# Adding the constant of the variance: a sum over pairs with a preset area in place of an addition with a scalar

## The reference, cut to what matters

```
def _layernorm(x, w, bias):
    mu = mean(x, -1);  var = mean(square(x - mu), -1)
    return (x - mu) * rsqrt(var + EPS) * w + bias          # EPS = 1e-5
def step(h):
    h = h + 0.01 * tanh(h)
    h = h * sigmoid(h)
    h = _layernorm(h, ln_w, ln_b)
    return einsum('bsc,dc->bsd', h, W) + b
x = x + scan(step, _layernorm(x), length=30)
```

## Time and profile before

| what | us |
|---|---|
| median of 3 runs (lowest, highest) | 1390.7 (1389.99, 1391.48) |
| the profiled execution's own time | 1390.53 |
| its span on the core | 1388.6 |
| DVE line 1116 in that span, 240 instructions | 107.3 busy, 0.447 each |

### The profile page before, as it was taken

How to read it: one execution, slowest core, us unless ns; L and a number is a source line. 1 busy time by engine, 2 the same in 40 slices (tenths; PEclk the granted TensorE clock), 3 DMA queues, 4 the chain that set the end, 5 groups by cost and what they waited for, 6 DMA issues and landing times.

```text
span 1388.6 us, 28231 instructions
## 1 busy us (share of the span) xinstructions
PE 1332.4 (96%) x8786; PEld 1085.0 (78%) x8786; DVE 1234.2 (89%) x2774; ACT 1011.1 (73%) x1373; POOL 948.3 (68%) x749
## 2 busy tenths in 40 slices
PE   4899999999999999869999999999999999999998
PEld 3677777777777776558888888888888888888887
DVE  6678888887788886599999999999999999999997
ACT  1344444444444444569999999999999999999994
POOL 2244444444444444269999999999999999999995
PEclk9899999999999999969999999999999999999999
DMA  5111111111111100000000000000000000000004
GB/s 178 39 39 38 38 38 38 38 38 38 38 38 38 37 0 1 0 1 0 0 0 0 0 0 0 0 0 0 0 0 0 0 0 0 0 0 0 0 0 122
DMA packets 29790, 27.68 MB, mean 20 GB/s; under 512 B 3269, under 2 KB 21448, under 8 KB 29640
## 3 DMA queue, kind: packets, MB, share of 16 engines
q1 hardware_dynamic: 29768, 27.41, 6.2%
HBM read 23.21 MB, written 4.19 MB: 20 GB/s over the span
## 4 chain that ended last, share of the span: by engine, by line
PE 78%; DVE 11%; issue 4%; ACT 3%; POOL 1%; SPq 1%; DMA 0%; DVEq 0%; ACTq 0%; POOLq 0%
PE psum L751 34%; PE psum L763 15%; PE psum L747 6%; PE psum L553 4%; PE psum L555 4%; PE psum L554 4%; PE psum L694 3%; PE psum L570 2%; PE psum L575 2%; ACT emb_f L855 2%; PE psum L584 2%; DVE emb_n L1177 1%; DVE x_less_n L1161 1%; PE psum L564 1%; DVE xh L1059 1%
## 5 line engine op out<-in xcount | busy, mean ns | idle before, releaser
L751 PE MATMUL psum<-w_t,y_all 128*128 128x128 f32 x3840 | 493.7, 282 | 0.0
L751 PEld LDWEIGHTS psum<-w_t,y_all 128*128 128x128 f32 x3840 | 447.9, 192 | 54.5 <-issue 54.5
L454 POOL TENSOR_TENSOR f_rs<-f_var,half_neg 128x8 f32<-128x8 f32 x240 | 410.4, 1710 | 49.2 <-DVE f_var L1116 30.2
L1091 DVE BATCH_NORM_STATS2 f_stat<-g_ring 128x6 f32<-128x256 f32 x960 | 340.7, 413 | 3.9 <-ACT g_ring L813 3.9
L458 POOL TENSOR_TENSOR h_ring<-g_ring,f_rs 128x640 f32<-128x640 f32 x240 | 302.5, 1260 | 18.8
L1107 DVE SCALAR_TENSOR_TENSOR u_ring<-t_ring,psum 128x1024 f32<-128x1024 f32 x232 | 278.1, 1199 | 0.0
L763 PE MATMUL psum<-ident,h_ring 128*128 128x128 f32 x1920 | 250.6, 274 | 6.4 <-DVE h_ring L1080 6.4
L813 ACT ACTIVATE g_ring<-u_ring 128x1024 f32<-128x1024 f32 x240 | 253.5, 1056 | 0.8 <-DVE u_ring L1107 0.8
L836 ACT ACTIVATE y_all<-psum 128x1024 f32<-128x1024 f32 x240 | 243.7, 1015 | 8.4 <-PE psum L763 8.4
L822 ACT ACTIVATE t_ring<-psum 128x1024 f32<-128x1024 f32 x232 | 238.6, 1029 | 13.5 <-PE psum L751 4.9
L763 PEld LDWEIGHTS psum<-ident,h_ring 128*128 128x128 f32 x1920 | 219.1, 142 | 7.1 <-issue 3.8
(11 more groups left out here) (158 smaller groups left out, 1774.3 us busy)
## 6 DMA issues: line engine op xcount, KB each, us to landing
work<-in_adj_dram SPq DMA_DIRECT2D x16, 1024.0 KB, 5.4
x_tok<-in_x_dram SPq DMA_DIRECT2D x16, 256.0 KB, 5.5
out_dram<-y_all SPq DMA_DIRECT2D x8, 512.0 KB, 3.3
work<-in_L_gnn_conv_w_dram SPq DMA_DIRECT2D x1, 1088.0 KB
work<-in_L_gnn_w_ih_dram SPq DMA_DIRECT2D x1, 384.0 KB
work<-in_L_gnn_w_hh_dram SPq DMA_DIRECT2D x1, 192.0 KB
work<-in_L_gnn_W_dram SPq DMA_DIRECT2D x1, 64.0 KB, 5.1
work<-in_L_ffn_weight_dram SPq DMA_DIRECT2D x1, 64.0 KB, 4.8
```

The costliest lines, as they stand in the source:

```text
L454: pool.tensor_tensor(f_rs[:, j % 4, :], f_var[:, j % 2, :], half_neg[:, 0:GT], ALU.pow).then_inc(f_pow, 1)
L751: m = pe.matmul(y_ps[k % 2][:, h, C * t:C * t + C], y_all[:, GT * k + NT * h + t, :], w1_t[:], start=False, stop=True, skip_group_check=True)
L1091: ins = dve.bn_stats(f_stat[:, j % 2, q, :], both)
```

## The change

The statistics area gets a second half of the same shape. At the start of the kernel the whole area is set to 128 * EPS (`C * EPS`), one more memset of 96 values per partition. The statistics instructions write only the first half, so the second keeps the constant. In each slot the addition with a scalar is replaced by a sum over the innermost axis of length 2: it reads, for each of the 8 tiles, the third value of the first half and the preset value of the second half, 16 values in all, and writes 8. The waits, the semaphores and the place in the order stay as they are.

```
-        f_stat = sb("f_stat", [P, 2, GT // 2, 6])
+        f_stat = sb("f_stat", [P, 2, 2, GT, 3])
...
             dve.memset(half_neg[:], -0.5)
+            dve.memset(f_stat[:], C * EPS)
...
-                        ins = dve.bn_stats(f_stat[:, j % 2, q, :], both)
+                        ins = dve.bn_stats(f_stat[:, j % 2, 0, 2 * q:2 * q + 2, :].rearrange("p t w -> p (t w)"), both)
...
-                    squares = f_stat[:, j % 2, :, :].rearrange("p q (o w) -> p (q o) w", w=3)[:, :, 2]
-                    dve.tensor_scalar(f_var[:, j % 2, :], squares, C * EPS, None, ALU.add).then_inc(f_v, 1)
+                    squares = f_stat[:, j % 2, :, :, 2].rearrange("p o t -> p t o")
+                    dve.tensor_reduce(f_var[:, j % 2, :], squares, AX_X, ALU.add).then_inc(f_v, 1)
```

## The result

| | before | after |
|---|---|---|
| median of the runs, us | 1391.09 (4 runs, 1389.99 to 1391.65) | 1380.37 (4 runs, 1379.24 to 1381.05) |
| the profiled execution, us | 1390.53 | 1381.05 |
| its span, us | 1388.6 | 1379.1 |

The ratio is 0.9923, its 95% interval [0.9906, 0.9940]: 10.7 us less, with 8.3 to 13.1 as the interval. The forecast was 1381.2.

The account below looks back on a forecast made before the run. A closed loop of POOL and DVE was taken to bound the kernel. From 1390.53, 27 x (25.765 - 25.42) = -9.3, rounded to -9.4, memset 0: 1381.1; the median 0.17 above: 1381.2 us, range 1379.5 to 1387.0.

Parts of the forecast that it names:

- TensorE's pace, seen in iteration 2, as the floor: Iterated stage: without waiting for DVE, TensorE runs every iteration at 25.42 us, 3.178 a slot, in place of 25.765.
- The hold by line 458: DVE's `f_var` addition waits until POOL's product (line 458) is over, 0.30 us of its 0.38 interval.
- The sum is not held, and takes 0.163 us: The new sum of 16 values on DVE passes beside line 458, held part 0, length 0.163 us.
- The first rival: The sum on DVE is held as the addition was: slot stays 3.24, 1391 to 1393 us, chance 0.10.
- The loop of POOL and DVE sets 25.76 us: The two engines wait for each other: seven slots of 3.24 us and one of 3.08 make the 25.76 us iteration.
- The hold passes to `h_ring`: DVE's `h_ring` (line 1080), behind the sum, is now held by line 458; DVE's slot becomes 2.94 to 3.12 us.
- POOL's loop at 3.05, between 2.94 and 3.17: POOL's power no longer waits for a held instruction, so POOL's slot is 3.05 us, under TensorE's 3.178.
- the second rival: Only part comes: POOL's power still waits some 0.15 us behind line 458, 1382 to 1390 us, chance 0.13.
- the third: Rival: POOL's power (line 454) queues behind both `h_ring` instructions, making it slower, 1399 us, chance 0.06.
- the lock-out: Rival: `h_ring` starting just as line 458 starts loses 1.1 us; if every second slot, about 1450 us, chance 0.01.
- The memset hidden: Start of kernel: 96 more values, 0.1 to 0.2 us, cost 0 behind DVE's 4.40 us wait for a transfer.
- A gain of 9.4 and not 72 us: The 240 holds of 0.30 us don't all count, since PE leaves room for only 0.043 us a slot.

Follow-up runs that it names:

- e3: Kernel before, scalar addition kept but its source laid out as 5 pairs with gaps (10 values): 1381.55 us, ratio 0.9931.
- e1: Kernel before, scalar addition replaced by an addition of two tensors, the statistics and a preset area of 8 values: 1390.23 us, ratio 0.9997.
- e4: Kernel before, scalar addition kept, but POOL's line 458 does 4 of 8 tiles in place of 5, DVE 3: 1380.65 us, ratio 0.9923.
- e8: Changed kernel with a longer sum, 128 values in all: 1391.4 us, ratio 1.0004 to the kernel before.
- e9: Changed kernel with a sum of 64 values in all: 1380.67 us, ratio 0.9923 to the kernel before.
- e5: Kernel before without the two bias products (line 747) on TensorE: 1387.91 us, ratio 0.9975.
- e6: Changed kernel without the two bias products (line 747) on TensorE: 1349.84 us, ratio 0.9705 to the kernel before.
- e12: Changed kernel with bias products moved behind the other 16, only each bank's first product starting a sum: 1371.87 us, ratio 0.9859 to the kernel before.

## Why the prediction was right

- **TensorE's pace, seen in iteration 2, as the floor.** Right to 0.01 us: 25.413 us an iteration from the second on, where the prediction had 25.42. It was the term that made the forecast: 27 x 0.345 = 9.3, taken as 9.4; measured 27 x (25.765 - 25.413) = 9.5. The other 1.2 us of the 10.7 lie in the medians: the profiled execution of the changed kernel is the longest of its four, and the kernel before has one run more and with it a median 0.4 higher than the one that the forecast started from.
- **The hold by line 458.** Right, and now shown from both sides: e3 removes it with the operation unchanged, e1 keeps it with another operation, e4 removes it by ending line 458 earlier.
- **The sum is not held, and takes 0.163 us.** Right: 0.170, never over 0.179. The first rival (the sum is held too) is out. That the length fits so well is partly luck: the prediction took 0.146 fixed and 1.04 ns a value from sums of neighbours, and e8 and e9 show 0.13 and 2.4 to 2.5 for this step, two errors that cancel at 16 values.
- **The loop of POOL and DVE sets 25.76 us.** Right: with less work for TensorE it keeps 25.77 (e5).
- **The hold passes to `h_ring`.** Right while DVE is behind. In iteration 1 the held instruction of before has become this pair, which begins 0.08 us behind the sum and is let go with POOL's line 458 (it ran 613.84 to 616.01):

```profile
614.82 0.17 DVE L1117 TENSOR_REDUCE f_var<-f_stat 128x8 f32<-128x16 f32 x1
614.90 1.38 DVE L1081 TENSOR_SCALAR h_ring<-g_ring,f_rs 128x128 f32<-128x128 f32 x2
```

  Its median length of 0.278 says that later it is mostly free or held for moments.
- **POOL's loop at 3.05, between 2.94 and 3.17.** The range held, as far as it can be seen: at TensorE's pace the power mostly takes 1.73, and 1.73 + 0.08 + 1.26 + 0.11 = 3.18 is TensorE's slot within the reading of these rows. When pressed (e6) POOL does 3.06 on the average and has idle time in it (574.48 busy of 600), so there was room and the second rival (part of it only) did not come. Nor did the third (the power behind both `h_ring`) or the lock-out as something that comes back: from iteration 2 to 30 no slot of TensorE is over 3.18.
- **The memset hidden.** Right: it takes 0.14 us, DVE still waits 3.72 us for the transfer behind its memsets, and iteration 2 starts 0.04 us later than before.

```profile
0.93 0.14 DVE L948 MEMSET f_stat<- 128x96 f32 x1
```

- **A gain of 9.4 and not 72 us.** Right in kind, and e6 adds what lies between: with less work on TensorE the same edit is worth 38 us, 27 x (25.77 - 24.50) = 34 of them in the iterations, where 3.06 a slot comes next, most likely ACT's.

## What to carry to other kernels

The instruction of 8 values that lasted 0.47 us was not slow, it was waiting: set such an instruction's end against the ends of the other engine's instructions before pricing its removal. Where two engines wait for each other in a ring, what one of them holds comes back as the pace of both, and either end of the ring can be cut: here the shape of one small operand, or a fifth of the neighbour's work. The gain is then what the next engine leaves, and a stretch of the same loop that already ran without the wait here showed that to 0.01 us an iteration. And what has room is bounded too: a sum of 0.290 us cost nothing here (e9), one of 0.446 took all of the gain back (e8).

## What the runs showed of the hardware that was not expected

- GpSimd's product (line 458) holds VectorE's addition of two tensors in SBUF, even for 8 values (e1: median 0.466, 0.152 at the least). The sum over pairs isn't held (0.179 at the most), nor is the scalar addition of 5 pairs (e3: 0.174 at the most). GpSimd's power (line 454), 1.64 us long, does not hold a scalar addition.
- In the stretches of before, after and e6 read here, the power takes 1.72 to 1.73 when it starts behind the second `h_ring` and 1.64 when it starts before it. That is no full rule: in e8 some take 1.81, as the one at 1000.30, beside the first of two `h_ring` instructions (a pair from 1000.15 to 1000.61):

```profile
1000.30 1.81 POOL L454 TENSOR_TENSOR f_rs<-f_var,half_neg 128x8 f32<-128x8 f32 x1
```

- A sum along a step of 96 bytes costs 2.4 to 2.5 ns a value (e8: 0.446 us for 128; e9: 0.290 for 64; after: 0.170 for 16) where a sum of neighbours costs 1.04.
- The order of TensorE's blocks alone is worth 0.04 us a slot: bias products behind the fp32 products, not ahead of them (e12).
